# A graph-attention and expert kernel: the split of the next masked rows one tile sooner, one load ahead of a store, and three subtractions moved to GpSimd

## The reference, cut to what matters

```python
xn = layernorm(x)
lQ, lK, lV = masked_x @ Wlq, xn @ Wlk, xn @ Wlv + blv
local  = where(adj, lQ @ lK.T / 16, -1e9)            # 4096 x 4096
glob   = (masked_x @ Wgq) @ (mean(xn) @ Wgk).T / 16  # 4096 x 1
es     = masked_x @ Wes
m      = max(max(local, axis=1), glob, es)
le, ge, ee = exp(local - m), exp(glob - m), exp(es - m)
den    = sum(le) + ge + ee
res    = le/den @ lV + ge/den * (mean(xn) @ Wgv + bgv) + ee/den * (masked_x @ Wev + bev)
x      = x + maximum(res, masked_x)
# second part: 8 experts, each on its own rows
h      = layernorm(x); a = (norm(h) * ln_g + ln_b) @ attn_w.T + attn_b + h
y      = gelu(a @ fc1[e].T + b1[e]) @ fc2[e].T + b2[e]
out    = x + gelu(y @ next_w.T + next_b)
```

## Time and profile before

| | us |
|---|---|
| runs of the kernel | 1088.25, 1088.60, 1088.91 |
| median | 1088.6 |
| the profiled execution | 1089.44 |
| its span, first to last instruction | 1087.6 |
| TensorE busy in it | 1041.1 (96%) |
| VectorE, GpSimd, ScalarE busy | 856.1 (79%), 706.8 (65%), 542.9 (50%) |
| mean granted TensorE clock | 0.992 |

### The profile page before, as it was taken

How to read it: one execution, slowest core, us unless ns; L and a number is a source line. 1 busy time by engine, 2 the same in 40 slices (tenths; PEclk the granted TensorE clock), 3 DMA queues, 4 the chain that set the end, 5 groups by cost and what they waited for, 6 DMA issues and landing times.

```text
span 1087.6 us, 15808 instructions
## 1 busy us (share of the span) xinstructions
PE 1041.1 (96%) x4996; PEld 869.1 (80%) x4996; DVE 856.1 (79%) x1532; ACT 542.9 (50%) x974; POOL 706.8 (65%) x717
## 2 busy tenths in 40 slices
PE   6878999999999999999999999999798999999998
PEld 5656887887887888788788788887687888888886
DVE  5889887797898789879879978987876775577653
ACT  5541444444444445344444444448566555655664
POOL 5764776777678677676767767768475455554451
PEclk9999999999999999999999999999899999999999
DMA  7585343453354345345425425449936647654621
GB/s 224 187 285 182 118 152 109 159 174 103 121 181 136 125 160 175 102 141 182 131 100 175 165 97 169 146 138 352 333 102 212 210 148 245 224 175 150 208 78 59
DMA packets 104341, 180.39 MB, mean 166 GB/s; under 512 B 14265, under 2 KB 45882, under 8 KB 104002
## 3 DMA queue, kind: packets, MB, share of 16 engines
q1 hardware_dynamic: 104258, 179.38, 49.2%
HBM read 143.63 MB, written 27.33 MB: 157 GB/s over the span
## 4 chain that ended last, share of the span: by engine, by line
PE 80%; DVE 6%; POOL 5%; issue 3%; DMA 3%; ACT 2%; SPq 1%; DVEq 0%; POOLq 0%; ACTq 0%
PE u_ps L1579 19%; PE s_ps L52 11%; PE s_ps L54 11%; PE s_ps L53 11%; PE u_ps L1586 9%; PE u_ps L52 2%; PE u_ps L54 2%; PE u_ps L53 2%; PE mt_ps L52 2%; PE mt_ps L53 2%; PE mt_ps L54 2%; POOL p_lo L713 2%; POOL m_lo L774 1%; PE mb_ps L52 1%; PE mb_ps L53 1%
## 5 line engine op out<-in xcount | busy, mean ns | idle before, releaser
L713 POOL TENSOR_TENSOR p_lo<-p_all,p_hi 128x512 fp32r<-128x512 f32 x224 | 295.7, 1320 | 172.1 <-PE u_ps L1586 104.9
L1309 ACT ACTIVATE p_hi<-scores 128x512 fp32r<-128x512 f32 x224 | 141.6, 632 | 358.8 <-DVE scores L886 358.5
L902 DVE TENSOR_TENSOR scores<-s_ps,bias 128x512 f32<-128x512 f32 x256 | 175.5, 686 | 85.5 <-PE s_ps L54 82.0
L1579 PE MATMUL u_ps<-p_hi,v_in 128*128 128x512 f32 x896 | 241.0, 391 | 0.0
L52 PE MATMUL s_ps<-q_hi,lnT_hi 128*128 128x512 f32 x512 | 202.5, 396 | 11.4 <-DVE scores L902 10.0
L53 PE MATMUL s_ps<-q_lo,lnT_hi 128*128 128x512 f32 x512 | 200.8, 392 | 0.0
L54 PE MATMUL s_ps<-q_hi,lnT_lo 128*128 128x512 f32 x512 | 200.7, 392 | 0.0
L1579 PEld LDWEIGHTS u_ps<-p_hi,v_in 128*128 128x128 f32 x896 | 167.2, 188 | 34.0
L705 POOL TENSOR_SCALAR bias<-adj 128x512 f32<-128x512 uint8 x256 | 164.9, 645 | 15.7 <-DVE scores L902 15.7
L886 DVE TENSOR_TENSOR scores<-scores,mb_ps 128x512 f32<-128x512 f32 x256 | 171.7, 676 | 0.8 <-PE mb_ps L1604 0.8
L923 DVE TENSOR_TENSOR kept_ps<-kept_ps,scores 128x512 f32<-128x512 f32 x232 | 162.2, 699 | 8.0
(11 more groups left out here) (216 smaller groups left out, 1770.9 us busy)
## 6 DMA issues: line engine op xcount, KB each, us to landing
v_in<-v_scratch SPq DMA_DIRECT2D x118, 512.0 KB, 3.6
adj<-in_adj SPq DMA_DIRECT2D x64, 256.0 KB, 3.9
raw<-in_wffn SPq DMA_DIRECT2D x32, 512.0 KB, 5.2
v_scratch<-vst SPq DMA_DIRECT2D x8, 1024.0 KB, 6.0
mx<-in_mx SPq DMA_DIRECT2D x18, 256.0 KB, 6.8
xg<-in_x SPq DMA_DIRECT2D x8, 512.0 KB, 4.6
uhi_scratch<-uT_high SPq DMA_DIRECT2D x8, 512.0 KB, 2.7
ulo_scratch<-uT_low SPq DMA_DIRECT2D x8, 512.0 KB, 3.6
```

The lines of the kernel that those rows point to most:

```text
L713: nc.gpsimd.tensor_tensor(out=low_part(y), in0=whole_part(y), in1=high_part(y).bitcast(fp32), op=ALU.subtract).then_inc(plo_ready, 1)
L902: nc.vector.tensor_tensor(scores[:, t % SLOTS], s_ps[t % 3][:, :], bias[:, t % 2], ALU.add).then_inc(masked, 1)
L1309: nc.scalar.activation(high_part(y), scores[:, y % SLOTS], ACT.Exp, scale=SCALE).then_inc(phi_ready, 1)
L1579: nc.tensor.matmul(u_ps[d][:, :], values[:, x % 2, at:at + P], high_part(x), start=k == 0 and part == 0, stop=False)
```

## The change

Seven places are edited; what is computed stays the same.

- In six attention blocks the split of the next masked rows stands one step sooner: `m_hi` on ScalarE at k = 21, `m_lo` on GpSimd at k = 22 and 23. Their load and the queries stay where they were.
- In `group(1)` of SP the load of masked rows stands ahead of the store of values.
- GpSimd makes the first two low weight matrices (`w_low`) at g = 2, not at g = 0.
- Low weights 15, 18 and 21 of the final block go from VectorE to GpSimd.
- In the final block the second `normalise` moves from i = 13 to 14, the first `low_normed` (`nT_lo`) from 16 to 15, the coefficients of block 6 from step 15 to 17, and their store on SP from 16 to 18.
- In expert 0 `shares` moves from j = 3 to j = 4.

```diff
@@ -365,7 +365,7 @@
             return TILES - SLOTS + slot + 4
 
         def is_late(y):
-            return y >= LAST + 4 and y % 3 == 2
+            return y >= LAST + 4 and y % 3 == 2 and y - LAST not in (15, 18, 21)
 
         def late_lows(y):
             return sum(is_late(i) for i in range(y))
@@ -586,13 +586,13 @@
                     if 0 < g < NG - 2:
                         sp.wait_ge(ln_ready, g + 1)
                         load_x(g + 2)
+                    if g == 1:
+                        sp.wait_ge(q_done, 2)
+                        load_masked(sp, 1)
                     if g > 0:
                         sp.wait_ge(vlo_ready, 2 * g)
                         sp.dma_start(v_dram[(g - 1) * TG:g * TG].rearrange("t p c -> p t c"),
                                      vst[:, (g - 1) % 2].bitcast(fp32)).then_inc(v_stored[(g - 1) % 2], 16)
-                    if g == 1:
-                        sp.wait_ge(q_done, 2)
-                        load_masked(sp, 1)
                     if 0 < g < NG:
                         sp.wait_ge(bias_ready, 4 * g)
                         load_adjacency(sp, g + 1)
@@ -658,7 +658,7 @@
                         sp.wait_ge(ulow_ready, 2 * ended + 2)
                         sp.dma_start(uhi_dram[ended], uT_high[:, :, :].bitcast(fp32)).then_inc(u_stored, 16)
                         sp.dma_start(ulo_dram[ended], uT_low[:, :, :].bitcast(fp32)).then_inc(u_stored, 16)
-                    ended = ended_since(t, 8, 16)
+                    ended = ended_since(t, 8, 18)
                     if ended is not None:
                         sp.wait_ge(coef_ready, 3 * ended + 3)
                         sp.dma_start(coef_dram[ended], coefs[:, 0:3]).then_inc(coef_stored, 16)
@@ -828,7 +828,7 @@
                         reciprocal_deviation(g + 2)
                     if 0 < g < NG:
                         bias_of(t + 5)
-                    if g == 0:
+                    if g == 2:
                         low_weight_matrix(0)
                         low_weight_matrix(1)
                     if g == 1:
@@ -844,8 +844,8 @@
                     for y in exponentials_in(t):
                         if not is_late(y):
                             low_weight(y)
-                    if k in (23, 24) and n + 1 < BLOCKS:
-                        low_queries_input(n + 1, k - 23)
+                    if k in (22, 23) and n + 1 < BLOCKS:
+                        low_queries_input(n + 1, k - 22)
                     for d in range(KD):
                         ended = ended_since(t, 1 + 2 * d, 9 + d)
                         if ended is not None:
@@ -1078,9 +1078,9 @@
                     if i in (9, 11):
                         residual(0, (i - 9) // 2)
                         moments(0, (i - 9) // 2)
-                    if i in (12, 13):
-                        normalise(0, i - 12)
-                    if i == 16:
+                    if i in (12, 14):
+                        normalise(0, (i - 12) // 2)
+                    if i == 15:
                         low_normed(0, 0)
                     if i in (24, 26):
                         extra_rows(BLOCKS - 2, range(i - 24, i - 22))
@@ -1125,7 +1125,7 @@
                             take_second(BLOCKS - 1)
                         if e > 0 and j in (1, 3):
                             last_bias(e - 1, j // 2)
-                        if e == 0 and j == 3:
+                        if e == 0 and j == 4:
                             shares(BLOCKS - 1)
                         if e == 0 and j in (6, 7):
                             extra_rows(BLOCKS - 1, range(2 * j - 12, 2 * j - 10))
@@ -1276,7 +1276,7 @@
                         extra_scores(n, (k - 6) // 6)
                         if k == 24:
                             top_extra(n)
-                    ended = ended_since(t, 6, 15)
+                    ended = ended_since(t, 6, 17)
                     if ended is not None:
                         shares(ended)
                     ended = ends_block(t - 10)
@@ -1532,7 +1532,7 @@
                         exponentials(y)
                     if n > 0 and k == 5 and n <= BLOCKS:
                         extra_weights(n - 1)
-                    if k == 22 and n + 1 < BLOCKS:
+                    if k == 21 and n + 1 < BLOCKS:
                         high_queries_input(n + 1)
                     if k in (26, 29) and n + 1 < BLOCKS:
                         high_queries(n + 1, k // 29)
```

## The result

The changed kernel takes **1080.34 us** (median of 3 runs, 1080.26 to 1081.32) against 1088.6: a ratio of 0.9925, 95% interval [0.9905, 0.9944]. That is 8.3 us less. I had forecast 1077.3 with a range of 1072.5 to 1083.0: the sign and the range hold, and the gain is 3 us smaller than my sum. In a second comparison the same kernel took 1079.01 against 1088.24, ratio 0.9919 [0.9904, 0.9934].

A forecast was written before the change was run, and what follows sets the result against it. TensorE, busy 96% of a 1087.6 us span, was taken as the bound, so only its standing or half-clock time could go. Terms -6.3 - 3.2 - 3.0 + 1.2 = -11.3 us gave 1077.3 us, range 1072.5 to 1083.

The forecast's parts named there:

- The split: Six attention blocks: splitting masked rows one tile sooner removes TensorE's stops for m_lo, 6.3 us gained, low bound 4.5.
- (d): Attention: ScalarE reaches the split before the masked rows land, so the kernel gets slower, 1091 from 14 us on; chance 0.02.
- (e): Query product waits as long for VectorE's extra scores as for m_lo, and the opening's lead is lost: 1086.8; chance 0.03.
- The load ahead of the store: Opening: masked rows land sooner and GpSimd's idle 1.77 and 1.43 us go, 3.2 us gained, bounds 0 and 4.
- rival (a): Only the attention blocks gain; the opening's head start is lost at the load of x: 1080.5; chance 0.13.
- rival (b): VectorE is held by GpSimd in the final block, gain there 0.5 and not 3.0 us: 1079.8; chance 0.15.
- The final block: VectorE loses 3.4 us of work ahead of nT_lo, so attend comes 3.0 us sooner; bounds 0.5 and 6.
- So I add 1.4 us: Final block: allowance for VectorE's second normalise running slower beside GpSimd's five low weights in a row.
- The rule of the Trainium skill: VectorE and GpSimd hold their shared SBUF port one at a time, a whole instruction each; final block gains the low bound.
- Rival (c): The clock stays up in the final block, where TensorE does tiles 15 to 18 without stops: 1074.4; chance 0.10.
- The coefficients: Expert 0: TensorE's 1.4 us at nT_lo is waited away at mT, whose load leaves later; 1.2 us lost, bounds 0 and 3.

The follow-up runs named there:

- lows_back: The changed kernel with the low weights of tiles 15, 18 and 21 of the final block back on VectorE: 1079.36 us, ratio 0.9921.
- coefs_earlier: The changed kernel with the coefficients of block 7 back at j = 3 of expert 0, ahead of nT_lo: 1079.44 us, ratio 0.9915.

## Why the prediction was right, and where it was not

**The split: right, in mechanism and size.** Forecast 6.3 us (six times 1.05), measured 6.42 in every kernel that has it. Nobody waits for `m_lo` or for VectorE's extra scores, `m_hi` has no wait for its load, and weighing to weighing is 4.07 us where I named 4.08. Rivals (d) and (e) are out.

**The load ahead of the store: right in mechanism, a little too large, and more than half of it not always kept.** Forecast 3.2 us from the two idle times of GpSimd. Measured up to the mean: 2.8 us by the changed kernel's profile, 2.0 to 3.1 over all profiles with this edit. The load of x moved with the chain, as I argued (issued at 59.20 and not 61.41, the wait behind it 2.97 us and not 2.94), so rival (a) as a mechanism is wrong, though its number, 1080.5, is the nearest to the result. The second comparison, 1079.01, is nearest to that of rival (b), 1079.8. The step that the sum lacked is that of the clock: I took the lead as kept from 98 us on, while behind TensorE's stop at the mean 1.6 us can be lost at 1.2 GHz, and were in the first profile. I treated the clock only in the final block.

**The final block: right sign, wrong sum.** Forecast 3.0 us at `attend`, measured 1.1. The 3.4 us taken from VectorE and the 1.0 us gained by the first normalise are right: that normalise took 1.29 us from start to the next instruction, against 2.27. Two steps failed.
- "So I add 1.4 us" for the second normalise. My own numbers, 4.1 against 2.3, make 1.8, so the 1.4 was a slip of working. The run shows 770.87 - 766.26 = 4.61 against 2.27 us, which is 2.3.
- I costed `x_next` at nothing. It also reads SBUF twice, and beside the low weight that moved to GpSimd it took 1.67 us in place of 0.69, another 1.0.

With both, 3.4 + 1.0 - 2.3 - 1.0 = 1.1. The kernel before had this quick `x_next` of the second half on VectorE

```profile
767.02 0.69 DVE L1018 TENSOR_TENSOR x_next<-resm,x 128x512 f32<-128x512 f32 x1
```

while its `x_next` of the first half, at 759.45 beside two of GpSimd's subtractions, took 1.67. The same instruction stood there at two prices, and I should have asked which one it would have after the move.

The rule of the Trainium skill that spoke against this part (SBUF — State Buffer, section "Who interferes with whom") went the right way. The durations of these runs agree with it: the same pair of VectorE instructions took 0.7, 1.7 or 2.6 us, steps of up to one GpSimd subtraction (1.3 us). I gave rival (b) a chance of 0.15 and 0.5 us of gain; what happened, 1.1, lies between it and my forecast, and nearer to it. For the move of the low weights alone it was right: lows_back shows no gain from it. Rival (c) is wrong, since the clock fell in all profiles of the changed kernel behind that stop.

**The coefficients: right in the wait, too large in the price.** Forecast: the 1.4 us at `nT_lo` is waited away at `mT`, and 1.2 us more. The first half is exact, and the 4.03 us wait for `h_lo` lies in the 3 to 5 that I named. The "1.2 us more" is 0 to 0.5 by coefs_earlier. My upper bound of 3 us was for a clock that falls behind the longer wait. It did fall (0.51 in the 3.5 us behind it), but in the kernel before it had fallen there too (0.67 behind 2.21 us of waiting), so this added next to nothing: from the `h_lo` matmul to the first `attend` of expert 1 it took 23.51 us, and 23.53 before. I had set the price by the delay of the store alone. The coefficients did start 1.2 us later relative to the work around them (7.5 us ahead of the kernel before, where that work was 8.7 ahead). But from there to the store it took 815.71 - 814.85 = 0.86 us and not 823.72 - 822.32 = 1.40, as their first addition took 0.15 us away from GpSimd's work and 0.69 beside it. So the store was only 0.7 us later.

**The sum.** By profile: 0.6 lost at the start (the first scores at 19.39 and not 18.75, a stretch that varies from 18.3 to 20.7 over all the kernels; 0.2 of it is five matmuls of the queries at half clock and not three, the rest a longer wait for ScalarE whose cause isn't shown), 2.8 in the opening, 1.6 lost behind the mean, 6.4, 1.1, and 0.0 in the experts: 8.1 us. Without the first and the third it would be 10.3, a microsecond from the 11.3 of the forecast. The second profile of the same kernel, where neither occurred, has a span 10.2 us below that of the kernel before. That the terms come so near is in part luck: the final block was 1.9 us too large and the opening 0.4, while the price of the coefficients was 0.7 to 1.2 too large the other way.

What stays open: why the clock falls in one execution behind the same stop and not in another. Also open is how the medians' distance from my sum divides: by the table 1.0 us is in the terms, and the 1.1 to 2.0 us left would be the clock's, which is a reading of 14 profiles and not a test.

## What to carry to other kernels

Before moving work from VectorE to GpSimd, add up what every VectorE instruction beside it will lose, not only the next one: here three subtractions moved and nothing was gained. Where an engine waits for a load, read the DMA queue for what stands ahead of it: taking a small store out of the way and putting the urgent load first shortened the experts by 4.3 to 4.7 us, of which some 1.4 us is work that no longer ran at half clock behind a wait. And cut every profile at the same few instructions: stretches that repeat to 0.1 us tell what an edit does even where medians scatter by 1 us.

## What the runs showed of the hardware

- TensorE at half clock comes by chance behind the same stop: behind 1.83 to 1.89 us of waiting for the mean came some 3.4 us at 1.2 GHz in 6 of 12 profiles, and none in the other 6. The cost was 1.6 us each time.
- Behind the 4.8 to 6.0 us stop of the final block the granted clock was 0.50 or 0.51 for the first 3 us of work in all ten profiles that have it, and between 0.50 and 1.00 in the next 3 us. From the first `attend` to the second took 7.4 to 8.9 us accordingly.
- The clock also fell in expert 0. In the 3.5 us behind the wait for `h_lo` the granted clock was 0.51 to 0.70 in the ten profiles where that wait was 1.80 to 4.37 us, and 1.00 in the two where it was 1.48 and 1.74 us. The same work then took 1.4 us less, before the waits for `nT_lo` that followed in those two.
- A pair of VectorE's 128x256 instructions of the normalise (`xn` or `xf`) took 0.72 or 0.73, 1.70 to 1.77, 2.15 or 2.61 to 2.76 us in the final block, by how much of GpSimd's row of 1.3 us subtractions ran beside it.
